# Attention by spectra on one Trainium2 core: keys' product first on TensorE, transposes by tile, x folded later, square root and exponential table loaded earlier

## The reference

```python
x = x + _L0_xattn_ref(_layernorm(x), ctx_4096, ctx_4096)      # H = 8, L = 256
x = x + _L0_ffn_ref(_layernorm(x), ...)
x = x + _L1_xattn_ref(_layernorm(x), ctx_4096, ...)
x = x + _L1_ffn_ref(_layernorm(x), ...)

def _autocorrelation(Q, K, V):
    qf = jnp.fft.fft(q, axis=2)
    kf = jnp.fft.fft(k, axis=2)
    corr = jnp.fft.ifft(qf * jnp.conj(kf), axis=2).real
    topk = int(C * np.log(L))                                # 11
    w, idx = jax.lax.top_k(corr.transpose(0, 1, 3, 2), topk)
    w = jax.nn.softmax(w, axis=-1)
    for i in range(topk):
        g = jnp.minimum(idx[:, :, None, :, i] + pos, L - 1)
        out = out + w[:, :, None, :, i] * jnp.take_along_axis(v, g, axis=2)
```

## Time and profile before

| | us |
|---|---|
| median of 3 runs (3222.43 to 3229.31) | 3222.8 |
| the profiled execution's own time | 3221.85 |
| its span | 3220.1 |
| PE busy, matmuls | 2921.2 (91%) |
| DVE busy | 2743.1 (85%) |
| ACT busy | 2258.1 (70%) |
| POOL busy | 1578.7 (49%) |

### The profile page before, as it was taken

The page is one execution under the profiler, slowest core; times in us unless marked ns, Lnnn a source line. Parts: engine busy times, 40 slices in busy tenths (PEclk is TensorE's granted clock), DMA queues, the critical chain, the costliest instruction groups (busy, mean ns, idle before and its releaser), DMA issues. The chain is left out here.

```text
span 3220.1 us, 47965 instructions
## 1 busy us (share of the span) xinstructions
PE 2921.2 (91%) x13554; PEld 1595.2 (50%) x13554; DVE 2743.1 (85%) x7168; ACT 2258.1 (70%) x5947; POOL 1578.7 (49%) x1161
## 2 busy tenths in 40 slices
PE   5999999999999996899999999999999999838886
PEld 3666666666666664445444454444445444412332
DVE  4999999999999997676888979788897978778996
ACT  6878888888888763665675857667586766467773
POOL 5899989998999994001212112121211212015776
PEclk8999999999999998999999999999999999859997
DMA  5555555555555544354564737456473744453664
GB/s 196 173 178 159 162 176 171 159 165 175 169 159 167 176 125 149 104 148 140 154 195 131 211 112 205 151 155 186 134 216 107 205 151 129 111 198 146 246 250 165
DMA packets 272044, 532.26 MB, mean 165 GB/s; under 512 B 32664, under 2 KB 132760, under 8 KB 248992
## 3 DMA queue, kind: packets, MB, share of 16 engines
q1 hardware_dynamic: 245600, 422.17, 42.0%
q10 hardware_dynamic: 15168, 71.34, 7.8%
q0 software_dynamic: 11008, 35.66, 3.3%
HBM read 401.07 MB, written 128.02 MB: 164 GB/s over the span
## 5 line engine op out<-in xcount | busy, mean ns | idle before, releaser
L1057 PE MATMUL acc<-xh,wq 128*128 128x512 f16 x4096 | 1204.5, 381 | 45.7 <-DVE x_first L1714 16.4
L1057 PE MATMUL acc<-xl,wq 128*128 128x512 f16 x2048 | 758.1, 380 | 0.0
L1276 ACT ACTIVATE unused<-c_first,minus_guess 128x256 bf16<-128x256 f32 x1024 | 505.2, 494 | 266.5 <-DVE minus_guess L1588 224.1
L1057 PEld LDWEIGHTS acc<-xh,wq 128*128 128x128 f16 x4096 | 399.2, 98 | 530.6 <-DVE x_first L1714 22.0
L986 POOL DMA_DIRECT2D c_first<-ctx_pairs x120 | 66.4, 554 | 859.1 <-DVE mk L1639 848.7
L1057 PEld LDWEIGHTS acc<-xl,wq 128*128 128x128 f16 x2048 | 200.9, 98 | 243.1 <-issue 2.5
L439 PEld LDWEIGHTS bu<-m_iz,zf 128*128 128x128 f32 x2048 | 278.9, 191 | 49.9 <-issue 35.2
L439 PE MATMUL bu<-m_iz,zf 128*128 128x128 f32 (+2 forms) x2048 | 293.0, 301 | 4.7 <-DVE zf L640 4.7
L458 PE MATMUL bx<-m_ic,pf 128*128 128x256 f32 x1024 | 239.5, 387 | 35.2 <-POOL pf L343 35.2
L458 PEld LDWEIGHTS bx<-m_ic,pf 128*128 128x128 f32 x1024 | 191.7, 192 | 70.9 <-POOL pf L343 46.9
L1258 ACT ACTIVATE unread<-cf 128x256 bf16<-128x256 f32 x256 | 106.1, 415 | 129.1 <-DVE feat_pair L1687 92.7
(11 more groups left out here) (358 smaller groups left out, 7019.3 us busy)
## 6 DMA issues: line engine op xcount, KB each, us to landing
wq<-w_split SPq DMA_DIRECT2D x512, 256.0 KB, 3.2
c_first<-ctx SPq DMA_DIRECT2D x64, 512.0 KB, 6.8
xt<-xT SPq DMA_DIRECT2D x64, 512.0 KB, 6.4
x_pairs<-xo SPq DMA_DIRECT2D x64, 512.0 KB, 3.3
c_first<-ctx_pairs POOLq DMA_DIRECT2D x128, 256.0 KB, 4.7
x<-xn_pairs SPq DMA_DIRECT2D x32, 1024.0 KB, 5.6
out_pairs<-ost SPq DMA_DIRECT2D x32, 1024.0 KB, 5.0
x_first<-x SPq DMA_DIRECT2D x15, 2048.0 KB, 7.6
```

What stands on the lines that cost most here:

```text
L1057: return pe.matmul(acc[b][:], ws[(WQ * o + k // CK) % WR][:, k % CK, a, :], x[:, k, :], start=start, stop=False)
L1276: act.activation(signs[:, u // 2, t] if n == COUNTS - 1 else unused[u % 2][:], ct[k % CR][:, t], ACT.Sign, bias=guess[q % 2][:, u:u + 1], ...
```

## The change

All of it is in the step functions of `attention_phase`.

1. PE: the spectrum of x (`spectrum_of_x`) is issued after the keys' product instead of ahead of it. Its waits go with it, and so do those of the keys' product.
2. PE: the eight transposes go tile by tile, two for each of the four tiles j of `wk`, each pair behind a wait for its own tile, instead of all behind one wait for the four.
3. POOL: `fold_x` comes after `spectrum_sum` (and so after `split_step`), in all steps but the first that has one.
4. ACT: the square root (`std`) goes from the end of step 3, between `w_back` and the first correlation copy, to step 0, ahead of the keys' copies; right behind it stands one exponential of one column, whose result nobody reads, so that the exponentials' table is loaded there.

```diff
--- before.py
+++ after.py
@@ -129,6 +129,7 @@
         total, negative = sb("x_total", [P, TT]), sb("minus_mean", [P, TT])
         parts, var = sb("var_parts", [P, TT, PIECES]), sb("var", [P, TT])
         std = sb("std", [P, TT])
+        warm = sb("exp_warm", [P, 1])
         rstd = sb("rstd", [P, TT])
         nmr = sb("nmr", [P, TT])
         bx, by, bz, bu = (pb(n, [P, 2, 512]) for n in ("bx", "by", "bz", "bu"))
@@ -152,6 +153,7 @@
         w_in = [sem(f"w0_in{i}") for i in range(2)]
         wn_in = [sem(f"w_rows_in{i}") for i in range(2)]
         w_out = [sem(f"w0_out{i}") for i in range(2)]
+        exp_ready = sem("exp_ready")
         w_scaled, w_hi, w_lo, w_summed, w_sums_out = map(sem, ("w0_scaled", "w0_hi", "w0_lo", "w0_summed", "w0_sums_out"))
         sq1_ok, halves_ok, chunk_ok, added_ok = map(sem, ("sq1_ok", "halves_ok", "chunk_ok", "added_ok"))
         N_CONST = 5
@@ -373,9 +375,12 @@
                 inverse_sums(it, k)
                 if it == 0 and k == AFTER_S:
                     fold_ctx(it, k)
-                fold_x(it, k)
+                if it == 0 and k == AFTER_S:
+                    fold_x(it, k)
                 split_step(it, k)
                 spectrum_sum(it, k)
+                if it or k != AFTER_S:
+                    fold_x(it, k)
                 if it or k != AFTER_S:
                     fold_ctx(it, k)
                 token_sums(it, k)
@@ -411,14 +416,14 @@
                 t = chunk(it, k, AFTER_T)
                 if f is not None:
                     kk = k - AFTER_F
-                    if least(f, 1):
-                        spectrum_of_x(f)
                     pe.wait_ge(ce_ok, 2 * (f + 1))
                     if least(f, 2):
                         pe.wait_ge(ze_mul, 2 * (f - 1))
                     elif f == 1:
                         pe.wait_ge(k_sb, 1)
                     folded(by, m_e, ce[kk % 2], k_mm)
+                    if least(f, 1):
+                        spectrum_of_x(f)
                     pe.wait_ge(eo_ok, f + 1)
                     if least(f, 2):
                         pe.wait_ge(zo_mul, 2 * (f - 1))
@@ -440,13 +445,13 @@
                     mm.then_inc(i_mm, 1)
                 if t is not None:
                     s = (k - AFTER_T) % 2
-                    pe.wait_ge(w_cut, CT * (t + 1))
                     if f is not None:
                         pe.wait_ge(dc_ok, f + 1)
                     else:
                         pe.wait_ge(ze_mul, 2 * t)
-                    for a in range(TT):
-                        for j in range(CT):
+                    for j in range(CT):
+                        pe.wait_ge(w_cut, CT * t + j + 1)
+                        for a in range(TT):
                             mm = pe.transpose(by[:, a, j * P:(j + 1) * P], wk[s][:, j, a * P:(a + 1) * P], ident[:])
                     mm.then_inc(t_mm, 1)
                 if f is not None:
@@ -562,6 +567,13 @@
                 split_step(it, k)
                 mean(it, k, 1)
                 squares(it, k, 1)
+                b = batch(it, k - CH)
+                if b is not None:
+                    act.wait_ge(ln_mv, b + 1)
+                    act.activation(std[:], var[:], ACT.Sqrt, bias=eps[:], scale=1.0 / D).then_inc(ln_std, 1)
+                    if least(b, 1):
+                        act.wait_ge(exp_ready, b)
+                    act.activation(warm[:], eps[:], ACT.Exp).then_inc(exp_ready, 1)
                 if f is not None:
                     s = (k - AFTER_F) % 2
                     act.wait_ge(k_mm, f + 1)
@@ -610,10 +622,6 @@
                     if least(t, 1):
                         act.wait_ge(fold_ok, 2 * t)
                     act.activation(wb[:], by[:, 1, :], ACT.Copy).then_inc(wb_sb, 1)
-                b = batch(it, k - 3)
-                if b is not None:
-                    act.wait_ge(ln_mv, b + 1)
-                    act.activation(std[:], var[:], ACT.Sqrt, bias=eps[:], scale=1.0 / D).then_inc(ln_std, 1)
                 if f is not None and least(f, 2):
                     act.wait_ge(w_cut, CT * (f - 1))
                 correlations(f, 0)
```

## The result

The changed kernel takes 3260.38 us, the median of four runs (3253.82 to 3263.55), against 3222.61 before (3221.12 to 3229.31, four runs with those of the first table). The ratio is 1.0106, 95% interval 1.0093 to 1.0119. A second comparison gave 3257.71 against 3224.45, ratio 1.0100 (1.0084 to 1.0117). The profiled execution took 3253.82 us, 32.0 more than the profiled one before, and its span is 3252.0 us.

The account below looks back on a forecast made before the run. Bound by a ring of waits over PE, DVE and POOL, a second close behind. Four steps change by 3 x 0.99 - 0.08 - 2 x 0.46 = +1.97 us, in all +30.5, giving 3253 us, range 3242 to 3266.

Parts of the forecast that it names:

- the ring over POOL's sums: Attention step: PE's correlation, DVE's `prod_e`, then 10.74 us of POOL, of which `fold_x` takes 2.5 us.
- E to B: From the end of `prod_e` to DVE's difference of `bu` and odd columns: forecast 10.53 us, before 9.54.
- the second ring: From `prod_e` through PE's products and inverse, ACT's odd columns and DVE back to `prod_e`: 9.54 and 9.21 us before.
- Part 1: Keys' product first on PE: it waits about 0.9 us for `prod_e`; steps 1 to 3 pay 0.99 us each.
- Part 2: Transposes by tile on PE: costed at nothing; without the inverse in front, at most 1.44 us saved.
- Part 3: Later `fold_x` on POOL: `pf` no longer waits for it; steps 1 and 3 gain 0.46 us each.
- the way back: From DVE's difference of `bu` and odd columns to the next end of `prod_e`: forecast 8.75 us, before 9.21.
- if the return path keeps its 9.21: Unfavourable bound on DVE's way back in the attention: steps 1 and 3 gain nothing, +14 us.
- Part 4: Root and two table loads of 1.28 us on ACT in step 0: hidden; PE's later inverse replaces a 0.95 us wait.
- the wait on `ze_mul` is met in time: PE reaches the keys' product with `prod_e` already done, so it does not stand: 3194 us; chance 5%.
- the ring stays as long as it was: Attention steps keep their length, gains and losses cancelling within 0.2%: 3223 us; chance 3%.
- a switch costs twice its row: An ACT table load right behind another activation costs twice 1.28 us: 3276 us; chance 4%.

Follow-up runs that it names:

- the product of x last: The changed kernel with the product of x behind the values' product too (keys, values, x, inverse): 3290.54 us, ratio 1.0211.

## Why the prediction was right, and where it was not

*What bounds.* The two rings were read rightly. The third edit alone shortens steps 1 and 3 by 0.46 us, which shows the ring over POOL's sums, and the other three edits without the first stop at E to B of 9.54 to 9.56 us, the length worked out for the second ring, through PE. The main signs named for the changed profile are there: PE's stand of 0.82 us for `prod_e`, L612's of 1.09, DVE's of 0.58 before L733, and steps of 19.35, 19.35, 19.81 and 19.35 us. DVE's stand of 0.73 us for the exponentials in step 1 was not forecast; it costs nothing, as said above.

*Part 1.* Right, and shown from both sides: alone it costs 1.4%, undone it turns +1.0% into -1.0%. Predicted were 10.53 us from E to B, measured are 10.605. The mis-sized term is the hand-over from DVE to PE, taken as 0.05 us and measured as 0.14 (708.11 to 708.25), less 0.02 on the pace after the stall. Over 62 steps that is 0.075 x 62 = 4.7 us, about the difference between the +30.5 forecast and the +34.5 us by which the last E came later. The rest of the 37.8 us between the medians is not in the profiled execution.

*Part 2.* Right: worth nothing. In the kernel before, POOL's `pf` covers it. With the keys' product in front the inverse does, in steps 1 to 3: the first edit alone still waits for all four tiles, and there the transposes show a stand in step 0 only:

```profile
686.91 1.09 PE L450 MATMUL by<-ident,wk 128*128 128x128 f32 x8
707.54 1.09 PE L450 MATMUL by<-ident,wk 128*128 128x128 f32 x8 [1.21 <-DVE wk L712]
```

To take that stand away gains nothing either, since with the second and third edits added no step changes. The second edit was not undone by itself in the changed kernel.

*Part 3.* The number was right, 8.74 us for the way back against 8.75, and its cause wrong. I wrote that steps 1 and 3 gain 0.46 us because `pf` no longer waits for the fold. The first edit alone has 8.74 with the fold in front, and undoing the fold's move in the changed kernel changes no step. With the keys' product in front, B comes 1.06 us later after E, and so do DVE's operations behind it, which PE's spectrum of the weights used to hold; they now find it ready. The first and the third edit each remove the same 0.46 us, and it can be had once. The bound "if the return path keeps its 9.21" could therefore not come true, whatever the fold did. That the term fitted the sum, although the edit that it was put down to gave nothing, was luck.

*Part 4.* Right: the loads make the keys' copies only 0.04 us later than in the next step, and step 0 no longer differs from 1 and 3 in E to B. Two of its terms were off and did no harm: ACT was free 0.83 us ahead of E (687.93 against 688.76) and not 0.27, and the last of the four operations ended at E + 2.27 (691.03), where "by E + 2.9" was forecast. Against the kernel with the first three edits it saves 0.6 us in step 0 (11.22 to 10.61), some 9 us in all; of the three further edits it is the one that counts there.

*The rivals.* That the wait on `ze_mul` is met in time: no, PE stands 0.82 us for it. The weights' spectra and `prod_e` do both start from DVE's fold, as said against it: in every version with the product of x ahead of the keys', the keys' product starts a median of 0.87 or 0.88 us after E without a stand, and in every one with the keys' in front PE stands 0.82 us in nearly all steps. That the ring stays as long as it was: no, four steps are 2.25 us longer. That a switch costs twice its row: no, two more places show 1.29 and 1.30 us. By the Trainium skill, "ScalarE: Activation LUTs", section "What ACT_TABLE_LOAD costs", each would have been 2.66 us, and the keys' copies an estimated 2.7 us later; the measurement decides against it here.

*The sum.* Single edits measured against the kernel before: +45.8, -2.2, -14.5 and -12.8 us. They add to +16.3, and the change took +37.8 (+33.3 in the second comparison). The steps show where the gap comes from. Four steps changed by +2.85, +0.02, -0.96 and -0.55 us, which add to +1.36, and the change made +2.25. The 0.89 between is the third edit's two times 0.46, which the first edit had already brought along; the second was worth nothing alone as well, and the fourth gives about the same in both places (0.55 and 0.59).

## What to carry to other kernels

Before putting a product in front, look at who last reads the buffer that it overwrites. The work that stood ahead of it may be what hides the wait for that reader. Moved behind the wait it no longer does, and everything that follows comes later by the stand. Follow each ring of waits (each closed chain of engines that wait for one another) separately and sum each. The longest sets the pace, gains on the others are worth nothing, and two edits that relieve the same wait are not worth their sum. If several edits come together, undo each one in the whole as well as doing it alone: here a version with three of the four was 2% faster than the whole.

## What was not expected of the hardware

The hand-over between the same two engines was not one number. PE started 0.05 us after the end of DVE's fold (722.35 + 0.68 = 723.03, PE at 723.08), but 0.14 us after the end of `prod_e` (708.11 to 708.25), and POOL too had started 0.14 us after it in the kernel before. With the product of x last, PE started the values' product 0.15 us after `prod_o`, of the same 1024 columns. No run here separates whether that lies in the operation's size, 1024 columns against 512, or in how its end is recorded.
